# Spectral layers of a small tower: the inverse along h for two pairs of images in eight tiles, with a second pair of PSUM banks

## The reference

```python
h = layer_norm(x @ fc0_w + fc0_b, ln0_g, ln0_b)          # 32 channels
for i in range(4):
    x1 = spectral_conv(h, w1[i], w2[i])   # rfft2, 12x12 modes at both ends of h mixed by channel, irfft2
    x2 = conv 1x1 of h with conv_w[i], plus conv_b[i]
    h = layer_norm(x1 + x2, ln_g[i], ln_b[i])
    if i < 3:
        h = gelu(h)
h = gelu(h @ fc1_w + fc1_b); h = gelu(h @ fc2_w + fc2_b); h = h @ fc3_w + fc3_b
```

## Time and profile before

| | us |
|---|---|
| median of 3 runs | 5699.33 |
| lowest, highest | 5688.65, 5706.58 |
| profiled execution | 5708.09 |
| its span | 5706.4 |

### The profile page before, as it was taken

The page is one execution under the profiler, slowest core; times in us unless marked ns, Lnnn a source line. Parts: engine busy times, 40 slices in busy tenths (PEclk is TensorE's granted clock), DMA queues, the critical chain, the costliest instruction groups (busy, mean ns, idle before and its releaser), DMA issues.

```text
span 5706.4 us, 135011 instructions
## 1 busy us (share of the span) xinstructions
PE 5290.3 (93%) x43556; PEld 2992.3 (52%) x43556; DVE 3978.1 (70%) x7712; ACT 3889.3 (68%) x6261; POOL 629.6 (11%) x943
## 2 busy tenths in 40 slices
PE   5888899999999999999999999999999999768878
PEld 3444556666666666666666654433333333334443
DVE  5888888888878888888888875555555555454453
ACT  5899776888666888666888666677777777523333
POOL 0133000333000333000333000000000000000000
PEclk9999999999999999999999999999999999878788
DMA  1344477666777676677666752221111111000000
GB/s 68 129 143 147 144 203 213 215 221 223 208 215 217 212 224 220 205 228 218 217 222 221 220 168 75 68 63 50 51 51 46 52 52 52 13 4 4 7 7 4
DMA packets 397185, 756.31 MB, mean 133 GB/s; under 512 B 245041, under 2 KB 303410, under 8 KB 331322
## 3 DMA queue, kind: packets, MB, share of 16 engines
q1 hardware_dynamic: 377402, 704.04, 39.0%
q0 software_dynamic: 19456, 48.01, 3.7%
HBM read 397.49 MB, written 354.42 MB: 132 GB/s over the span
## 4 chain that ended last, share of the span: by engine, by line
PE 82%; DVE 7%; issue 5%; ACT 4%; SPq 1%; DMA 0%; ACTq 0%; DVEq 0%
PE ps_y L914 18%; PE ps_y L907 9%; PE ps_t L926 9%; PE ps_t L1017 8%; PE ps_t L935 8%; PE ps_f L948 4%; PE ps_f L1002 4%; PE ps_s L893 3%; PE ps_s L961 3%; PE ps_f L987 3%; PE ps_t L1026 2%; PE ps_t L346 2%; PE ps_y L883 2%; ACT big L1170 1%; PE ps_f L336 1%
## 5 line engine op out<-in xcount | busy, mean ns | idle before, releaser
L1147 ACT ACTIVATE big<-ps_y 128x512 f32<-128x512 f32 x1280 | 780.4, 610 | 756.9 <-PE ps_y L914 705.7
L914 PEld LDWEIGHTS ps_y<-conv_now,big 128*128 128x128 f32 x8192 | 993.5, 191 | 521.0 <-issue 521.0
L1310 DVE TENSOR_REDUCE big<-big 128x16 f32<-128x512 f32 x1280 | 853.2, 680 | 568.8 <-ACT big L1147 568.3
L1303 DVE TENSOR_TENSOR big<-big 128x512 f32<-128x512 f32 x1280 | 1008.3, 806 | 203.5 <-PE ps_t L926 201.3
L914 PE MATMUL ps_y<-conv_now,big 128*128 128x128 f32 x8192 | 1147.5, 283 | 0.0
L1156 ACT ACTIVATE big<-ps_t 128x512 f32<-128x512 f32 x1024 | 625.1, 610 | 326.3 <-PE ps_t L935 320.7
L926 PE MATMUL ps_t<-ident,big 128*128 128x128 f32 x5120 | 789.9, 277 | 26.5 <-DVE big L1303 25.3
L1163 ACT ACTIVATE big<-ps_t,g_now 128x512 f32<-128x512 f32 x1024 | 811.0, 792 | 4.9 <-PE ps_t L926 4.1
L1151 ACT ACTIVATE big<-ps_y 128x512 f32<-128x512 f32 x1280 | 783.6, 612 | 0.0
L926 PEld LDWEIGHTS ps_t<-ident,big 128*128 128x128 f32 x5120 | 585.5, 141 | 247.2 <-issue 206.5
L935 PE MATMUL ps_t<-ident,big 128*128 128x128 f32 x4096 | 653.5, 282 | 63.6 <-ACT big L1156 63.6
(11 more groups left out here) (180 smaller groups left out, 6228.8 us busy)
## 6 DMA issues: line engine op xcount, KB each, us to landing
hstore<-big SPq DMA_DIRECT2D x256, 1024.0 KB, 4.0
big<-hstore SPq DMA_DIRECT2D x256, 1024.0 KB, 5.3
xmodes<-x_out SPq DMA_DIRECT2D x128, 312.0 KB, 4.4
y_kt<-ymodes SPq DMA_DIRECT2D x512, 78.0 KB
ymodes<-y_st SPq DMA_DIRECT2D x192, 144.0 KB, 3.1
mix_room<-xmodes SPq DMA_DIRECT2D x48, 336.0 KB, 7.2
mix_room<-xmodes SPq DMA_DIRECT2D x48, 288.0 KB, 6.2
ymodes<-y_st SPq DMA_DIRECT2D x64, 192.0 KB, 3.4
```

The costliest lines, as they stand in the source:

```text
L914: last = mm(ps_y[:, wh, 128 * b:128 * b + 128], h_in[k // 2][:, at:at + 128], conv_now[:, :], start=False, stop=(b == 3))
L1147: af(y_sq[wh], ps_y[:, wh, :], ACT.Square).then_inc(s["sq_done"], 1)
L1303: v_.tensor_tensor(groups(xhat[wh]), groups(y_sb[2 * k + wh]), rstd[:, k // 2, at:at + 16].unsqueeze(2).to_broadcast([128, 16, 32]), ALU.m ...
L1310: v_.tensor_reduce(ss[:, k // 2, at:at + 16], groups(y_sq[wh]), AX.X, ALU.add).then_inc(s["ss_done"], 1)
```

## The change

In slots of the layer phases, and in the first quad of the head phase (`both`):

- `inv_h` runs at k 0 and 2 only, for both pairs: 8 matmuls in 32x64 tiles, those of the odd slot into ps_f, which now is the second pair of banks for y; `conv`, `square` and `keep_y` of odd slots use ps_f. `inv_h` waits for y_read of all slots before.
- `fwd_h` writes ps_s, and stands behind the slot's first `turn_back` and `turn_out`, just ahead of `inv_h`; it waits for the turn that empties ps_s.
- `inv_w` moves from the end of slots 0 and 2 to slots 1 and 3, behind the first `turn_out`, and waits for `turn_w`; `fwd_w` moves ahead of slot 1's second `conv`.
- `mix` writes ps_y instead of ps_f, behind `inv_w`, and waits until ps_y has been read.
- VectorE's turning steps and `mix` come behind the two scalings of their slot; `turn_modes` moves from slot 2 to slot 1, between the two `sums`.
- xhat is gone: `normed` scales y_sb in place and no longer waits for the transpose; `keep_y` waits for t1_done in place of xhat_done.

Head slots get the in-place scaling and the same waits, and otherwise stay as they are.

```diff
         y_sq = [carve(512) for _ in range(2)]
-        xhat = [carve(512) for _ in range(2)]
         h_px = [carve(512) for _ in range(4)]
         ss, rstd = (carve(128).rearrange("p (j n) -> p j n", j=2) for _ in range(2))
         var, nt = carve(64), carve(64)
...
+        def y_of(odd, both):
+
+            return ps_f if both and odd else ps_y
...
-            def inv_w(n, j, fw_count, to):
+            def inv_w(n, j, fw_count, tw_count, to):
 
                 i = n - QUADS
                 wait(pe, "y_loaded", 64 * i + 64)
                 wait(pe, "iw_read", 2 * i + j)
                 wait(pe, "fw_read", fw_count)
+                wait(pe, "tw_done", tw_count)
...
-            def inv_h(n, k):
-
-                j, odd, i = k // 2, k % 2, n - QUADS
-                if odd == 0:
+            def inv_h(n, k, both):
+
+                j, i, odds = k // 2, n - QUADS, (0, 1) if both else (k % 2,)
+                if k % 2 == 0:
                     wait(pe, "iw_read", 2 * i + j + 1)
                     wait(pe, h_loaded[j], 16 * i + 16)
                 wait(pe, "y_read", 2 * (4 * n + k))
-                for image in range(2):
-                    for wh in range(2):
-                        r, half = slice(64 * image + 32 * wh, 64 * image + 32 * wh + 32), image ^ odd
-                        mm(ps_y[64 * half:64 * half + 64, wh, :].rearrange("p (w o) -> p o w", o=32), c_inh[r, :],
-                           z_kx[j][r, :].rearrange("p (o w) -> p o w", w=32)[:, :, 16 * odd:16 * odd + 16], start=True, stop=False)
-
-            def conv(k, wh):
+                for odd in odds:
+                    for image in range(2):
+                        for wh in range(2):
+                            r, half = slice(64 * image + 32 * wh, 64 * image + 32 * wh + 32), image ^ odd
+                            mm(y_of(odd, both)[64 * half:64 * half + 64, wh, :].rearrange("p (w o) -> p o w", o=32), c_inh[r, :],
+                               z_kx[j][r, :].rearrange("p (o w) -> p o w", w=32)[:, :, 16 * odd:16 * odd + 16],
+                               start=True, stop=False)
+
+            def conv(k, wh, both):
 
                 for b in range(4):
                     at = 512 * (2 * (k % 2) + wh) + 128 * b
-                    last = mm(ps_y[:, wh, 128 * b:128 * b + 128], h_in[k // 2][:, at:at + 128], conv_now[:, :],
+                    last = mm(y_of(k % 2, both)[:, wh, 128 * b:128 * b + 128], h_in[k // 2][:, at:at + 128], conv_now[:, :],
                               start=False, stop=(b == 3))
                 last.then_inc(s["y_done"], 1)
 
...
                     wait(pe, "tok_done", tok_before)
                 for b in range(4):
-                    last = nc.tensor.transpose(ps_t1[:, 128 * b:128 * b + 128], xhat[wh][:, 128 * b:128 * b + 128], ident[:, :])
+                    last = nc.tensor.transpose(ps_t1[:, 128 * b:128 * b + 128], y_sb[2 * k + wh][:, 128 * b:128 * b + 128], ident[:, :])
                 last.then_inc(s["t1_done"], 1)
...
-            def fwd_h(m, j, mixed):
+            def fwd_h(m, j, to, mixed, iw_count, fw_count, y_count):
 
                 then(pe, "px_done", 8 * m + 4 * j + 4)
                 then(pe, "tw_done", 2 * m + j)
                 then(pe, "mix_read", mixed)
+                then(pe, "iw_read", iw_count)
+                then(pe, "fw_read", fw_count)
+                then(pe, "y_read", y_count)
...
-                            last = mm(ps_f[at:at + 32, odd, :], c_fwh[r, :], h_px[2 * odd + wh][r, :], start=True, stop=True)
+                            last = mm(to[at:at + 32, odd, :], c_fwh[r, :], h_px[2 * odd + wh][r, :], start=True, stop=True)
...
+            def mix(part, chunk, seq, ph, k, count, tw_count, to, free):
 
                 k0 = PARTS[part][0]
                 if k == 0 and part == 0 and chunk == 0:
@@ -975,7 +984,7 @@
                     else:
                         pe.wait_ge(x_half[part // 2], 64 * (3 * (ph if chunk == 1 else ph - 1) + chunk))
                 wait(pe, "tw_done", tw_count)
-                wait(pe, "g1_done", g1_count)
+                wait(pe, "y_read" if to is ps_y else "g1_done", free)
...
                         mixed = mixed + 2
-                    if k == 0 and back2 in STORED:
-                        fwd_h(n - 2, 1, mixed)
-                    if k == 2 and back1 in STORED:
-                        fwd_h(n - 1, 0, mixed)
                     inner = back1 == "head"
+                    both = front in MIXED and not inner
+                    if k == 0 and back2 in STORED and not both:
+                        fwd_h(n - 2, 1, ps_f, mixed, 0, 0, 8 * n if inner else 0)
+                    if k == 2 and back1 in STORED and not both:
+                        fwd_h(n - 1, 0, ps_f, mixed, 0, 0, 0)
...
                         visit = (part, chunk, seq, ph, k - 1, count, tw_count)
-                    if visit is not None and not inner:
-                        mix(*visit, 0)
+                    if visit is not None and front == "stem":
+                        mix(*visit, ps_f, 0)
...
-                        inv_h(n, k)
-                        conv(k, 0)
+                            wait(pe, "tw_done", 2 * n - 3)
+                        if k == 0:
+                            fwd_h(n - 2, 1, ps_s, 0, 2 * i + 1, 0, 0)
+                        if k == 2:
+                            fwd_h(n - 1, 0, ps_s, 0, 0, n - 1, 0)
+                        if k % 2 == 0:
+                            wait(pe, "mix_read", mixed)
+                            inv_h(n, k, True)
+                        if k == 1:
+                            inv_w(n, 1, 0, 2 * n - 2, ps_s)
+                        if k == 3 and nxt in MIXED:
+                            inv_w(n + 1, 0, 0, 2 * n - 1, ps_s)
+                        if visit is not None:
+                            mix(*visit, ps_y, 2 * (4 * n + k))
+                        conv(k, 0, True)
                     if back1 in STORED:
                         turn_back(turned - 1, k, 1)
                     if kind is not None:
-                        turn_out(turned + 1, kind, 1, 0)
+                        turn_out(turned + 1, kind, (k + 1) % 4, 1, 0)
+                    if k == 1 and back2 in STORED and both:
+                        fwd_w(n - 2, 2 * i + 2, 0)
                     if front in MIXED:
-                        conv(k, 1)
-                    if k == 0 and front in MIXED:
-                        inv_w(n, 1, n - 2, ps_s)
-                    if k == 1 and back2 in STORED:
-                        fwd_w(n - 2, 2 * i + 2 if front in MIXED else 0, 0)
-                    if k == 2 and nxt in MIXED:
-                        inv_w(n + 1, 0, n - 1, ps_s)
+                        conv(k, 1, True)
+                    if k == 1 and back2 in STORED and front == "stem":
+                        fwd_w(n - 2, 0, 0)
+                    if k == 2 and nxt in MIXED and front == "stem":
+                        inv_w(n + 1, 0, n - 1, 0, ps_s)
...
-            def square(unit, wh):
+            def square(unit, wh, of):
                 act.wait_ge(s["y_done"], unit + 1)
                 wait(act, "ss_done", unit - 1)
-                af(y_sq[wh], ps_y[:, wh, :], ACT.Square).then_inc(s["sq_done"], 1)
-
-            def keep_y(unit, k, wh):
-                wait(act, "xhat_done", unit - 7)
-                af(y_sb[2 * k + wh], ps_y[:, wh, :], ACT.Copy).then_inc(s["y_read"], 1)
+                af(y_sq[wh], of[:, wh, :], ACT.Square).then_inc(s["sq_done"], 1)
+
+            def keep_y(unit, k, wh, of):
+                wait(act, "t1_done", unit - 7)
+                af(y_sb[2 * k + wh], of[:, wh, :], ACT.Copy).then_inc(s["y_read"], 1)
...
-            def turn_w(m, j):
+            def turn_w(m, j, of):
                 wait(dve, "f_done", 2 * m + j + 1)
                 wait(dve, "fw_done", m)
-                v_.transpose(t_w[:, j, :].rearrange("p (c k) -> p c k", k=32), flat(ps_f).rearrange("p (w c) -> p c w", c=32)
+                v_.transpose(t_w[:, j, :].rearrange("p (c k) -> p c k", k=32), flat(of).rearrange("p (w c) -> p c w", c=32)
                              ).then_inc(s["tw_done"], 1)
...
             def normed(unit, half, k, wh):
                 dve.wait_ge(s["y_read"], unit + 1)
                 dve.wait_ge(s["norm_step"], NEWTON * (half + 1))
-                wait(dve, "t1_done", unit - 1)
                 at = 16 * (2 * (k % 2) + wh)
-                v_.tensor_tensor(groups(xhat[wh]), groups(y_sb[2 * k + wh]),
+                v_.tensor_tensor(groups(y_sb[2 * k + wh]), groups(y_sb[2 * k + wh]),
                                  rstd[:, k // 2, at:at + 16].unsqueeze(2).to_broadcast([128, 16, 32]), ALU.mult
                                  ).then_inc(s["xhat_done"], 1)
...
                         continue
-                    if k == 0 and back2 in STORED:
-                        turn_w(n - 2, 1)
-                    if k == 2 and back2 in STORED:
```

(50 more changed lines are left out.)

29 lines of the change are left out of this document (14 added, 15 removed).

## The result

The changed kernel takes 5642.42 us (median of 5 runs, 5639.71 to 5657.21), the kernel before 5699.33 (5 runs beside it, 5685.57 to 5706.58): ratio 0.9907, interval 0.9890 to 0.9924. It is faster, by 57 us, a third of the 175 us that were forecast, and its time lies 17 us above the range. The profiled execution spans 5640.7 us against 5706.4.

What follows compares the result with a forecast made beforehand. TensorE was taken to bound the layer quads until VectorE or ScalarE takes over. 48 weight quads x (25.4 - 24.6) plus 49 mixing quads x (27.8 - 25.0) save 175 us, giving 5525 us; range 5460 to 5625.

Steps and rivals of the forecast that it cites:

- rival of two rounds: TensorE's inv_h: eight tiles run in two rounds, 0.86 us more twice per quad, 5631 us in all; chance 0.12.
- ScalarE's burst: End of slot 1 in weight quads: copies 1.1, signs 2.8, px 0.5, together 4.4 us; alone makes about 24 us.
- one hold that stays: Weight quads: GpSimd's first addition likely still holds a VectorE scaling, the second perhaps not; 1.5 holds taken.
- VectorE's idle time in slot 1: VectorE idles 1.3 us before turn_modes, waiting for fwd_w, and some 0.6 before the second sums; closed in mixing quads.
- ps_s handshake: Rival "slower": fills of ps_s exposed on VectorE, up to 6.9 us per quad; with three, 5800 us; chance 0.05.
- 0.3 for single late waits: Mixing quads: 0.3 us added to TensorE's 24.7, giving 25.0.
- removed islands: Differently tiled groups on TensorE fall from eight to five per quad, saving 3 x 0.17 = 0.5 us.
- one late wait: TensorE's 0.48 us gap ahead of fwd_h of slot 0 goes, as ScalarE's copy has 0.9 us more.
- 25.4 - 3.1 = 22.3 us: TensorE's sum for a weight quad after savings of 2.1, 0.5 and 0.48; 24.7 for a mixing quad.
- overlaps with VectorE's bound and adds a little: 24.6: Weight quads: ScalarE's about 24 us combined with VectorE's own loop of 24.5 us gives 24.6.
- stay at 25.4: Stated sign of being wrong: weight quads keep the 25.4 us they took in the kernel before.
- main case: Weight quads 24.6 us, mixing quads 25.0, 175 us saved, 5525 us; spans 5495 to 5570; chance 0.52.

Runs made afterwards that it cites:

- e3: Changed kernel with inv_h back in four matmul groups of 4, each slot's ahead of its own conv: 5826.19 us, ratio 1.0228 to the kernel before.
- e7: Kernel before with only the scaling in place, its wait for t1_done gone and keep_y waiting for it instead: 5702.93 us beside 5704.53, ratio 1.0001.
- e9: Changed kernel with ScalarE's copy of y for a slot's first half moved behind the second half's gelu, in layer slots: 5603.54 us.
- e5: Changed kernel with ScalarE's weight scaling cut to 4 of 144 elements and GpSimd's addition to 12 of 576, in the layers: 5616.49 us.
- e8: Changed kernel, all work done, with ScalarE's weight signs spread behind gelus and GpSimd's additions started only after two scalings: 5617.82 us.
- e1: Changed kernel with only ScalarE's scaling of new weights (sign_w1, sign_w2) cut to 4 of 144 modes in the layers: 5668.85 us.
- e11: Changed kernel, all work done: copy of y late, weight signs spread, additions paced, VectorE's turning steps ahead of the scalings again: 5524.52 us.
- e2: Changed kernel with only GpSimd's weight addition cut to 12 of 576 elements in the layers: 5651.25 us.

## Why the prediction was wrong

**Right.** Inv_h in eight tiles costs 1.05 us where 1.0 was taken, and saves 2.0 per quad (e3). The rival of two rounds, and the rule of the Trainium skill with it (TensorEngine Tiling (Array Packing), Restrictions and Gotchas), would have given 1.9 for a group; the 1.05 leaves no room for a second round, so two row tiles write one bank at once here, against that rule. The time alone would have misled: that rival's 5631 us, with 26.7 and 25.1 for the quads, lies nearest to the measured one, by coincidence. The in-place scaling costed at nothing is nothing (e7). ScalarE's burst (4.6 for 4.4), one hold that stays and VectorE's idle time in slot 1 (1.3 and 0.6) are as said. Not slower: of the ps_s handshake 0.19 us per weight quad is exposed, ahead of fwd_w (1900.72), and nothing in the mixing quad shown.

**Wrong, the mixing quads: 1.9 of 25.0, some 93 us of 49 quads.** The step that failed is the term "0.3 for single late waits" that was added to TensorE's sum: three borders of 0.5, 1.5 us, stand there. I had priced the removed islands as cost alone (0.5) and the one late wait (0.48) as cured by 0.9 of delay. But an island at a border is also cover for ScalarE's 2.4 us from conv to gelu, against which TensorE has 2.2. The 16.9 us that ScalarE is busy in 24.7 hid that: not its load but its latency through two single banks decides. e9 shows it: 0.5 less on ScalarE's way, and the waits at the borders are gone.

A smaller part is the sum itself, "25.4 - 3.1 = 22.3 us". The pieces of a mixing quad's chain without the mix, between two turn_outs (2339.25 to 2366.24, mix 2.83), come to 24.2, and without the 1.5 to 22.7. Of the 0.4 over 22.3, some 0.15 is fwd_h (1.02 and 1.08, where I kept the 0.86 that it had right behind fwd_w), 0.1 is inv_h (1.07 and 1.05 for 1.0), and 0.1 the five changes of shape, 0.2 each. Together: 1.2 for the borders beyond the 0.3, 0.4 for the sum, and 0.3 by which the mean lies above the chain, most of it the 38.4 us before the head; that makes the 1.9.

**Wrong, the weight quads: 0.64 of 24.6, some 31 us.** The terms held, their combination didn't. I took the burst ("about 24") and VectorE's 24.5 as overlapping. But the burst's 24 was summed against a TensorE chain without the borders' waits: with them that chain is 24.44 (e5, e8), and the burst adds 0.8. VectorE's bound lies right beside it: with the burst gone both additions hold and its loop is 25.6 (e1). So the step that failed here is "overlaps with VectorE's bound and adds a little: 24.6", again for want of the borders' waits. The sign "stay at 25.4" was all but met. VectorE's 84% instead of 93% comes from the longer quad, the one hold for 1.5, and a sum that was too high: 23.4 per quad with two holds was said to fit the windows' 22.3, and it doesn't; the changed kernel's windows give 21.2 with one.

**Sum.** 93 and 31 make 124 us. For the profiled execution 5533 + 124 = 5657; less the 14 us of the tail and the 2 of the stem, which weren't forecast, 5641 for the 5642 measured. One recorded sum is wrong by itself: with 23.7 and 24.7 us for the quads the main case begins at 5465 us (48 x 1.7 + 49 x 3.1 = 234), not at 5495; the range held it all the same.

**What stays open.** Why the granted clock in the tail differs from run to run. That e11 comes to 5524.5 is no late confirmation of 5525: its weight quads are far below the forecast (23.1 for 24.6), its mixing quads above it. Which load holds the mixing quads of e9 to e11, and why turns behind the scalings cost 1.0 there and 0.2 in the changed kernel, other than that another bound lay just above, was read from chains alone.

## What to carry to other kernels

When a step is moved off a tightly pipelined place, ask what it covered: an engine that hands over through single banks needs the consumer's whole latency (here 2.4 us) between two visits, however low its busy share. Two bounds side by side show nothing when one is removed (e1 and e2 gave nothing or less, e5 gave 0.8), so take them away together before calling either harmless. And where one engine's work holds another's, pace it by a wait for the moment when it meets an operation that it can't hold (e8), rather than letting its inputs time it.

## What the runs showed of the hardware

A hold doesn't go by the size of the operation that is held: GpSimd's fp32 addition of 576 elements kept a step of VectorE on 64 elements for 1.75 us instead of 0.23 (e1), and a scaling for 1.7 more, while the transpose from PSUM beside it took its 1.24 (e8), and a sum beside the changed kernel's second addition (1914.86) its 0.64. The Trainium skill (SBUF — State Buffer, Who interferes with whom) says that a VectorE instruction with two SBUF inputs contends with a GpSimd instruction that reads SBUF, that one with at most one SBUF input, outside its two-port modes, doesn't, and that the order of issue, not the shape of the operation, decides who blocks. The trace agrees: in e1 the addition ran from 1908.08 to 1910.01, and the step, issued 0.26 behind it, ended at 1910.09.

Eight 32x64 tiles, four of them into each of ps_y and ps_f, ran in 1.05 us, the four of before in 1.02. And a late hand-over costs more than its lateness: at a border gelu ended 0.15 us behind the point at which turn_out could have started, yet the pair of transposes took 0.5 more, 0.2 in each piece (0.64 and 0.63 for 0.44) and 0.1 between them. Why a piece takes 0.63 there isn't shown.
